# Softmax bound of the next unit: where TensorE turns it, and which engine's queue carries it through HBM

## The reference

```python
xn = _layernorm(x)
q, k, v = (proj(W) for W in (Wq, Wk, Wv))          # 16 heads of 32
q, k = _apply_rope(q, k)
scores = einsum('bhqd,bhkd->bhqk', q, k) / sqrt(32)
attn = softmax(where(causal, scores, min), axis=-1)
att = einsum('bhqk,bhkd->bhqd', attn, v) ... @ Wo.T
w, top_idx = softmax(top 2 of xn @ gate_w.T)
ffn = sum over the 2 experts of w * (xn @ expert_w[e].T + expert_b[e])
return x + att + ffn
```

## Time and profile before

| | |
|---|---|
| median of 3 runs | 984.97 us (984.73 to 988.17) |
| the profiled execution's own time | 987.53 us |
| its span, first to last instruction | 985.8 us |
| TensorE busy | 917.9 us, 93% of the span |
| VectorE, GpSimd, ScalarE busy | 744.3, 561.3, 436.6 us |
| mean granted TensorE clock | 0.987 of full |
| chain that ended last | TensorE 66%, VectorE 14%, DMA 6%, ScalarE 5%, GpSimd 4% |

### The profile page before, as it was taken

The page is one execution under the profiler, slowest core; times in us unless marked ns, Lnnn a source line. Parts: engine busy times, 40 slices in busy tenths (PEclk is TensorE's granted clock), DMA queues, the critical chain, the costliest instruction groups (busy, mean ns, idle before and its releaser), DMA issues.

```text
span 985.8 us, 18723 instructions
## 1 busy us (share of the span) xinstructions
PE 917.9 (93%) x6557; PEld 452.1 (46%) x6589; DVE 744.3 (76%) x1327; ACT 436.6 (44%) x711; POOL 561.3 (57%) x553
## 2 busy tenths in 40 slices
PE   2898898999999989989999999989999999999887
PEld 1344344444444544545555555544444444444333
DVE  7988988898789899944444444487788888888865
ACT  5367867766765433431122111124334444344432
POOL 1545676674776446763333333157878888778731
PEclk9999999999999999999999999999999999999999
DMA  6365589688786353485655555464655554565531
GB/s 243 109 223 198 179 269 320 199 306 293 211 275 260 119 204 97 187 291 192 198 176 178 172 171 174 148 214 141 193 177 188 172 194 141 163 189 159 173 103 55
DMA packets 107963, 188.63 MB, mean 191 GB/s; under 512 B 11872, under 2 KB 65248, under 8 KB 102624
## 3 DMA queue, kind: packets, MB, share of 16 engines
q1 hardware_dynamic: 97072, 152.03, 44.4%
q0 software_dynamic: 10800, 35.40, 12.5%
HBM read 117.13 MB, written 70.25 MB: 190 GB/s over the span
## 4 chain that ended last, share of the span: by engine, by line
PE 66%; DVE 14%; DMA 6%; ACT 5%; POOL 4%; issue 3%; SPq 1%; another core or an unknown queue 0%; DVEq 0%; ACTq 0%; POOLq 0%
PE psum L949 19%; PE psum L1034 10%; PE psum L1058 7%; PE psum L997 5%; PE psum L984 5%; PE psum L966 5%; PE psum L1000 5%; PE psum L1043 4%; PE psum L926 4%; DVE top L1483 3%; ACT pT L762 2%; DMA sum_sb<-x 2%; POOL k_hl L590 1%; PE psum L968 1%; DMA w_rows<-w_hl 1%
## 5 line engine op out<-in xcount | busy, mean ns | idle before, releaser
L762 ACT ACTIVATE pT<-psum,factors 128x512 f32<-128x512 f32 (+1 forms) x352 | 218.2, 642 | 244.0 <-PE psum L984 226.8
L1483 DVE TENSOR_REDUCE top<-psum 128x1 f32<-128x384 f32 (+3 forms) x352 | 210.4, 634 | 22.0 <-PE psum L968 16.6
L1034 PE MATMUL psum<-xT,w_att 128*128 128x512 f16 x768 | 195.7, 380 | 6.7 <-DVE xT L1434 4.7
L949 PE MATMUL psum<-w_exp,x_gT 128*128 x852 | 195.3, 379 | 0.6 <-DVE x_gT L1439 0.6
L610 POOL DMA_INDIRECT x_g<-xn_rows,tok_of x71 | 67.5, 951 | 131.5 <-PE psum L926 129.6
L966 PE MATMUL psum<-k_stack,q_stack 96*128 96x384 f16 (+3 forms) x512 | 127.8, 303 | 15.6 <-DVE top L1483 13.0
L984 PE MATMUL psum<-q_stack,k_stack 98*128 98x256 f16 (+3 forms) x512 | 129.5, 306 | 11.0 <-ACT pT L762 8.9
L1439 DVE TENSOR_TENSOR x_gT<-psum,x_gT 128x512 f16<-128x512 f32 x71 | 49.0, 692 | 104.1 <-ACT x_gT L786 90.7
L949 PEld LDWEIGHTS psum<-w_exp,x_gT 128*128 128x128 f16 x852 | 83.4, 98 | 85.5 <-issue 0.9
L786 ACT ACTIVATE x_gT<-psum 128x512 f16<-128x512 f32 x71 | 42.3, 597 | 170.0 <-PE psum L926 170.0
L600 POOL TENSOR_TENSOR o_hl<-o_sb,o_hl 128x512 f16<-128x512 f32 x31 | 36.5, 1178 | 127.9 <-ACT o_hl L776 123.2
(11 more groups left out here) (175 smaller groups left out, 1301.9 us busy)
## 6 DMA issues: line engine op xcount, KB each, us to landing
y_rows<-y_sb SPq DMA_DIRECT2D x71, 256.0 KB
w_in<-w_all SPq DMA_DIRECT2D x12, 1024.0 KB, 12.1
q_stack<-qk_rows SPq DMA_DIRECT2D x96, 128.0 KB
k_stack<-qk_rows SPq DMA_DIRECT2D x96, 128.0 KB
x_in<-x SPq DMA_DIRECT2D x8, 1024.0 KB, 10.2
qk_rows<-q_hl SPq DMA_DIRECT2D x32, 256.0 KB
qk_rows<-k_hl SPq DMA_DIRECT2D x32, 256.0 KB
xn_rows<-x_in SPq DMA_DIRECT2D x8, 1024.0 KB, 5.0
```

The costliest lines, as they stand in the source:

```text
L762: act.activation(p_of(j, h, heads), banks[BANK_T + (NT_ * n + k) % 2][:, 0:W], ACT.Exp, scale=factors[:, 0:1]).then_inc(exp_done, 1)
L949: now = pe.matmul(banks[s % 4], x_gT[s % 4][:, xp * C + c, :], w_exp[:, bass.ds(e, 1), wp, c, :].rearrange("p e d -> p (e d)"), start=n == ...
L1034: now = pe.matmul(bank, w_att[:, what, wp, c, g * P:(g + 1) * P], xT[b % 2][:, xp * C + c, :], start=at_pass == 0, stop=at_pass == 3 * C - 1)
L1483: return dve.tensor_reduce(out=top[:, h:h + heads, i], in_=banks[BANK_S + k % 2][:, 0:heads * W].rearrange("p (h t) -> p h t", h=heads), a ...
```

## The change

TensorE's `turn_c(n + 1)` moves from ahead of `shifted_scores` 9 to between `times_v(n, 0)` and `times_v(n, 1)`, so `scores(n + 2, 0)`, which doesn't use bank 1, no longer waits for the copy. ScalarE's `copy_c` moves behind the exponentials of pieces 9 and 10 (in the six steps with `high_x`, between its third and its fourth part), waits for its own copy and issues the store; a new `load_c`, still later in the step, waits until the store has landed and issues the load. SyncE's `move_c` is gone.

```diff
-            def move_c(m):
-                sp.wait_ge(c_copied, m + 1)
-                sp.dma_start(c_rows[m]..., c_turn[:]).then_inc(c_stored, 16)
-                sp.wait_ge(c_stored, 16 * (m + 1))
-                sp.dma_start(q_stack[m % 3][ROW_C:ROW_C + 2, :, :]..., c_rows[m]).then_inc(c_loaded[m % 3], 16)
...
                 act.activation(c_turn[:], half(BANK_S + 1)[0:2 * HG * J, 0:P], ACT.Copy).then_inc(c_copied, 1)
+                act.wait_ge(c_copied, m + 1)
+                act.dma_start(c_rows[m]..., c_turn[:]).then_inc(c_stored, 16)
+
+            def load_c(m):
+                act.wait_ge(c_stored, 16 * (m + 1))
+                act.dma_start(q_stack[m % 3][ROW_C:ROW_C + 2, :, :]..., c_rows[m]).then_inc(c_loaded[m % 3], 16)
...
                 exps(n, 8)
-                if n + 1 < N:
-                    copy_c(n + 1)
                 if n + 3 < N:
                     high_qk(1, n + 3)
...
                 if n in TURN_AT:
                     high_x(TURN_AT[n], 2)
+                if n + 1 < N:
+                    copy_c(n + 1)
+                if n in TURN_AT:
                     high_x(TURN_AT[n], 3)
                 if n in STATS_AT:
                     std_of(STATS_AT[n])
+                if n + 1 < N:
+                    load_c(n + 1)
                 if n in JOB_AT:
                     sum_w(JOB_AT[n])
...
             copy_c(0)
             take_v(1, V_FIRST[1])
             std_of(1)
+            load_c(0)
...
-                elif m:
+                elif k and m:
                     pe.wait_ge(c_copied, m)
...
-                if nxt:
-                    turn_c(n + 1)
                 shifted_scores(n, 9)
...
                 if nxt:
                     times_v(n, 0)
+                    turn_c(n + 1)
                     times_v(n, 1)
```

More of the change, by code:

```diff
@@ L410, in stack @@
                     sp.dma_start(to[u][place_no * HD:(place_no + 1) * HD, :, :], rows[half_no]).then_inc(done[u], 16)
-            def move_c(m):
-                sp.wait_ge(c_copied, m + 1)
-                sp.dma_start(c_rows[m].rearrange("f (r t) -> (f r) t", t=P), c_turn[:]).then_inc(c_stored, 16)
-                sp.wait_ge(c_stored, 16 * (m + 1))
-                sp.dma_start(q_stack[m % 3][ROW_C:ROW_C + 2, :, :].rearrange("p h s -> p (h s)"), c_rows[m]).then_inc(c_loaded[m % 3], 16)
             def load_early(w):
@@ L463, in _ @@
             store_qk(0, 2)
-            move_c(0)
             store_qk(1, 2)
@@ L499, in _ @@
                     store_x(NORM_AT[n])
-                move_c(n + 1)
                 store_qk(1, n + 3)
@@ L769, in copy_c @@
                 act.activation(c_turn[:], half(BANK_S + 1)[0:2 * HG * J, 0:P], ACT.Copy).then_inc(c_copied, 1)
+                act.wait_ge(c_copied, m + 1)
+                act.dma_start(c_rows[m].rearrange("f (r t) -> (f r) t", t=P), c_turn[:]).then_inc(c_stored, 16)
+            def load_c(m):
+                act.wait_ge(c_stored, 16 * (m + 1))
+                act.dma_start(q_stack[m % 3][ROW_C:ROW_C + 2, :, :].rearrange("p h s -> p (h s)"), c_rows[m]).then_inc(c_loaded[m % 3], 16)
             def high_o(n):
```

## The result

The changed kernel took 1000.49 us in the median of 10 runs (992.47 to 1004.2), the kernel before 987.09 us in 10 runs beside it (984.73 to 992.76). The ratio is 1.0122 with a 95% interval of 1.009 to 1.0153: slower by 1.2%, where I had forecast 0.2% faster and a range that ended at 989.5 us. The profiled execution is the slowest of the ten, 1004.2 us (987.53 before), so its differences add up to 16.7 us where the medians say 13.4.

What follows compares the result with a forecast made beforehand. TensorE, busy 93% of the span, was taken as the bound, with at most 11.0 us at `turn_c` to win. Terms -1.2 - 1.3 - 0.5 - 0.6 + 0.35 + 0.25 + 0.6 = -2.4 from 984.97 gave 982.6 us, range 976 to 989.5.

Steps and rivals of the forecast that it cites:

- The new wait: ScalarE waits in `load_c` for the store's landing, ahead of `sum_w` in nine steps: +0.6 us, ends 0 and 6.
- ScalarE's issues: ScalarE issues 32 stores and 32 loads, mostly hidden: +0.35 us in the preamble, +0.25 us in step 1.
- the third rival: Slow stores of c make ScalarE hold the row sum, `spread_max` and step 15's copy of x_g: 990.5 us, chance 17%.
- The 0.9 us that I had called spare: Slack between the row sum of w and TensorE's arrival at `spread_max`, with an undisturbed store of 1.4 us.
- the threshold of 2.3 us: Landing time of the store of c from which each further us holds the row sum, then `spread_max`.
- My sign for the slow side: Forecast wrong on the slow side if `sum_w` starts over 3.5 us after c's copy, or ScalarE's issue takes a us.
- c loaded in time: c needs 3.3 us from the new turn, TensorE reaches `shifted_scores` after 6.6: 3.3 us spare, costs nothing.
- The turn later: Turn 3.1 us later covers TensorE's waits at `turn_c`: -1.2 us in step 8, -1.3 us in step 15.
- SyncE without c: SyncE's transfers behind c go sooner, ending VectorE's wait for `sum_sb` in step 7: between 0 and 0.9, taken as -0.5 us.
- k's copy first: ScalarE copies k ahead of c, 0.16 us sooner, in four steps on GpSimd's chain: -0.6 us.
- GpSimd starts first: Rival: GpSimd's k_hl starts before VectorE's w_hl, winning 2.06 us in three steps, -6.2 us more: 976.4 us, chance 14%.
- The late steps stay at 20.81 us: In late steps TensorE works 20.75 of 20.81 us from turn to turn; no gain was expected there.

Runs made afterwards that it cites:

- both parts undone: Changed kernel, but SyncE waits for the landing and loads c, and ScalarE copies k behind c in steps 13 and 14: 986.87 us, 0.9987 of the kernel before.

## Why the prediction was wrong

**The new wait, +0.6 us with 6 as its end.** This is the first term that was mis-sized. Of its parts, ScalarE's issues held (309 and 236 ns). The way from store to load was 1.9 to 2.8 us in most steps up to 16 instead of 1.4 (and some 4.1 in three, in two of which ScalarE also waited for VectorE). In most late steps it is 1.36 us on ScalarE's queue and 1.38 on SyncE's: I had taken one landing at 57 us for all, though the earlier trace rows has 65.7 us in 29 waits, 2.3 us each. In five of the steps the copy began 0.9 us or more behind the turn instead of 0.25, since ScalarE was still busy (`high_x` at 126.66 above). TensorE waited 7.4 us at `spread_max`, and the whole change of load and wait is worth 0.78%, 7.7 us. I had the mechanism in the third rival, and gave it 17% because SyncE's stores of 8.5 us had stood behind bulk. What I didn't ask is how long such a store takes once SyncE no longer waits for it: I had counted SyncE's freedom only as a gain, and of five kernels that store c from ScalarE at the same place, the landing is slow in the two where SyncE is free.

The 0.9 us that I had called spare, and so the threshold of 2.3 us, were not there in step 2, from which I had read them. The 8.3 us from turn to `spread_max` hold a stretch at the lower clock (granted 0.79 from 119.96 to 128.28), behind the turn's own wait of 1.69 us; in the kernel before:

```profile
122.07 1.95 PE L1000 MATMUL psum<-pT,ones 128*32 128x512 f32 x8
```

In a late step the same eight products take 1.04 us. In the changed kernel TensorE is there 4.2 us after the turn in step 2, against my 5.2, and no landing of more than 1.4 us would have been free. In steps 4 to 9, which have a part of `project_out` in between, it is there after 5.1 us.

Two sums were wrong as well. An end of 6 us for this term, with no gain from the others, makes +6.6, and not the +1.5 with which the forecast's own range ends. And the third rival's price, by its own terms, is 982.6 plus the 2.5 us of gains that are gone plus 10, some 995 us and not 990.5. My sign for the slow side, `sum_w` over 3.5 us after the copy of c, never came: it was 2.0 to 3.4 us, since the copy was late too.

**c loaded in time, costs 0.** This step failed outright, and the 3.3 us spare are from a late step. I moved the copy of c behind the copy of k and priced only what k gains, 0.16 us. That ScalarE waits 7.92 us there for GpSimd in step 13 stood in the trace of before; c had been ahead of that wait. The copy came 7.1 and 5.0 us after the turns of these two steps, and TensorE waited 2.08 us for the copy and 4.10 us for the load. Putting k behind c gives 0.52% back with ScalarE's load and 0.46% with SyncE's (1.004 to 0.9994).

**The turn later, -1.2 and -1.3 us.** The waits at the turn went but for one, and others took their place. In the kernel with the late turn and SyncE's transfers TensorE waits for exponentials between 60 and 440 us as in the first row; in the kernel before 3.8 us, of which none was above 0.7:

```profile
PE psum L984 <- ACT pT L761: 15.0, 17, 2.8
PE psum L966 <- DVE top L1482: 8.8, 7, 2.6
PE psum L966 <- ACT c_turn L768: 2.2, 2, 1.9
```

The 10.5 us of waits for c_hl in that stretch came back as 11.2 for exponentials (15.0 less 3.8), and with k behind c as well these waits are still 14.1 us. With both parts undone the kernel is at 0.9987, where the 2.1 us of the late steps alone would make 0.9979; so the late turn won nothing in the early steps that a run here can tell. Half of each wait was still too much. Up to the experts only step 15 gave something back in this trace: the first expert started 20.5 us after the step's first exponentials (449.19 and 428.72) instead of 21.3 (432.22 and 410.93), 0.8 us and not 1.3.

**SyncE without c, -0.5 us, and k's copy first, -0.6 us.** What I said of SyncE's queue came true: its store of k in step 7 goes at 249.02, 0.03 us after GpSimd's end (247.82 + 1.17), and no wait for the blocks of x is left. It was worth nothing that can be measured (the interval reaches from -1.8 to +1.1 us), since the kernel with ScalarE's transfers at the old places took 0.9997. The rule of the Trainium skill that I had weighed against it (DMA: Bandwidth & Descriptors, Issuing engines are not separate DMA queues), by which nothing is won in steps 7 and 8, fits this better than my reading of the row. k's copy first: 1.0007.

**GpSimd starts first.** The rival came true in its mechanism and not in its price. I counted what k_hl wins and not that gT, the next of GpSimd, then waits for w_hl: 3.23 + 1.15 us before, 1.17 + 3.2 after, the same 4.4. The Trainium skill (SBUF — State Buffer, SBUF: two separate sides) says that who starts first holds the port pair for its whole instruction and the other blocks; the lengths here agree, and the rule, carried on to the next instruction, would have told me that nothing is won.

**The late steps stay at 20.81 us.** They don't. Counted from one start to the next, TensorE's matmul records show the turn taking 0.16 us at its old place and 0.01 at the new one, and the products of `project_out` take 0.09 us less too. The loads of weights fit that; first the kernel before and then the changed one, at the turns of 728.86 and 729.32:

```profile
728.86 0.09 PEld L973 LDWEIGHTS psum<-ident,c_hl 128*32 128x32 f16 x1 [0.42 <-DVE c_hl L1493]
729.02 0.11 PEld L984 LDWEIGHTS psum<-q_stack,k_stack 98*128 98x128 f16 x2
```

```profile
728.90 0.10 PEld L972 LDWEIGHTS psum<-ident,c_hl 128*32 128x32 f16 x1 [0.30 <-issue]
728.90 0.12 PEld L996 LDWEIGHTS psum<-pT,v_sb 128*32 128x32 f32 x3
```

At the old place the turn's load starts when its matmul does, and the load of the 128 columns behind it 0.16 us later. Between the products the next loads, of 32 columns like the turn's, go out with it, 0.42 us ahead. That c_hl was only just ready is not the reason: in step 13 before it was ready 1.4 us ahead of the turn (372.05 and 373.42), and the load still starts with its matmul, the next one 0.16 us later. That the turn next to the products on one side is enough (20.57 us) was shown; that it is the change of width that costs is the reading that fits, not shown alone.

**What I left out.** The clock. 5.7 of the 15.9 us in steps 0 to 14 are matmuls at the lower level, in the six stretches behind waits of 2.1 to 2.4 us or two shorter ones together. I had priced a wait at its length, and read a distance from a slowed stretch.

Of steps 0 to 14 nothing was gained, so the sum -2.4 us should have read about -2 (late steps) + 5 (k in steps 13 and 14) + 8 (load and wait) = +11, against 12 measured. The 5 and the 8 are from the runs, not from the traces I had. 1.9 us of the profiled run's difference lie ahead of step 0, 1.4 of them ahead of the first turn, where the change had issued nothing yet; the runs don't explain these.

## What to carry to other kernels

Before an instruction is moved down an engine's queue, read what the engine waits for between the old place and the new one, in every step and not in the smoothest: the wait of 7.92 us that c had been ahead of stood in the trace. A wait for a DMA's landing is priced by landings in the crowded stretch, and belongs on an engine that has nothing else to do; the store alone could go to ScalarE for nothing. An engine that waits also holds back what stands behind it in its queue: before it is freed, ask what its transfers will meet. Where TensorE is the bound, a new wait may be paid again by its clock: all five waits of 2.08 to 4.10 us in steps 0 to 15 of the changed kernel were.

## What the hardware did that I had not expected

- A turn with 32 columns of weights costs TensorE 0.23 us a step between work with 128 columns, and next to nothing beside products with 32: 20.81 against 20.58 us.
- A block at the port pair is handed on: in either order k_hl and the first gT took 4.4 us together, only w_hl changed, 2.30 or 3.30 us.
- The small store of c took 1.36 us to be seen landed in the late steps and 1.9 to 2.8 in most early ones from ScalarE's own queue, with nothing ahead of it there. From the same queue it took under 1.4 in nine of sixteen steps where SyncE waited for c before it went on to k. An own queue didn't keep this small transfer free of the others; the order in which the two queues start did.
- A wait of 4.10 us for c was followed by a stretch at the lower clock in which six products took 2.77 us instead of 1.46.
